# Eight of 56 precomputed parts moved from the traces of block 0 to its tails, in a fused four-layer residual kernel

## What is computed

```python
# layer 0: gated multi-scale traces
wg     = sigmoid(concat(x, ema(x)) @ Wg + bg);  gated = x * wg
h1     = gelu(x @ Wn1 + bn1)                     # 64 wide
mod    = 0.5 + sigmoid(h1 @ Wn2 + bn2)           # 16 numbers for each token
traces = [ema_d(gated * mod[:, d]) for d in range(16)]
gate   = sigmoid(sum_d(traces[d] * blend[d]) @ Wtemp + btemp)
soma   = gelu(x @ Wsoma + bsoma)
x      = x + layernorm((soma * gate) @ Wout)
# layer 1: tanh scores, masked softmax over tokens, pooling
x      = x + softmax(mask + tanh(x @ W1 + b1) @ v) @ x / count
# layer 2: eight gated experts and a shared one (SiLU), all of them for every token
# layer 3: x + gelu(x @ W1 + b1) @ W2, with an expert's columns picked for each sequence
```

## Time and profile before

| | us |
|---|---|
| median of the three runs | 2813.46 |
| their lowest and highest | 2812.75, 2815.56 |
| the profiled execution, its own time | 2811.08 |
| its span in the trace | 2809.3 |
| TensorE busy | 2771.3 (99%) |
| VectorE, ScalarE, GpSimd busy | 1786.2, 1450.2, 1207.1 |

### The profile page before, as it was taken

How to read it: one execution, slowest core, us unless ns; L and a number is a source line. 1 busy time by engine, 2 the same in 40 slices (tenths; PEclk the granted TensorE clock), 3 DMA queues, 4 the chain that set the end, 5 groups by cost and what they waited for, 6 DMA issues and landing times.

```text
span 2809.3 us, 36696 instructions
## 1 busy us (share of the span) xinstructions
PE 2771.3 (99%) x12794; PEld 2301.0 (82%) x12794; DVE 1786.2 (64%) x2976; ACT 1450.2 (52%) x2625; POOL 1207.1 (43%) x950
## 2 busy tenths in 40 slices
PE   8799999999999999999999999999999999999999
PEld 5588888888888888888888888888888888888888
DVE  8698778867777666566765766555766563333443
ACT  4455666566456544554545644455644563333445
POOL 5256435633554345424543345433454333333334
PEclk9899999999999999999999999999999999999999
DMA  4244333433222322112321222211322131111221
GB/s 154 73 151 127 97 105 105 142 99 102 80 68 95 111 68 68 57 59 68 105 64 59 81 89 73 68 48 57 111 79 63 44 103 45 46 45 46 79 89 58
DMA packets 117383, 230.37 MB, mean 82 GB/s; under 512 B 13672, under 2 KB 58960, under 8 KB 117200
## 3 DMA queue, kind: packets, MB, share of 16 engines
q1 hardware_dynamic: 81808, 190.15, 21.3%
q10 hardware_dynamic: 32832, 29.49, 4.3%
q0 software_dynamic: 2560, 8.39, 0.9%
HBM read 219.89 MB, written 8.09 MB: 81 GB/s over the span
## 4 chain that ended last, share of the span: by engine, by line
PE 94%; DVE 4%; issue 1%; ACT 1%; DMA 0%; SPq 0%; ACTq 0%; DVEq 0%
PE bank L587 20%; PE bank L588 20%; PE bank L589 20%; PE ps_out L587 10%; PE ps_out L589 10%; PE ps_out L588 10%; PE bank L580 1%; DVE trace L1137 1%; DVE trace L1129 1%; PE bank L708 0%; DVE w_lo L1209 0%; PE bank L699 0%; DMA pre_x<-in_xT 0%; PE bank L694 0%; DVE hid L1243 0%
## 5 line engine op out<-in xcount | busy, mean ns | idle before, releaser
L1382 POOL TENSOR_TENSOR hid_lo<-hid,hid_hi 128x512 fp32r<-128x512 f32 x640 | 848.3, 1326 | 1547.7 <-ACT hid_hi L1014 1547.3
L587 PE MATMUL bank<-res_lo,w_hi 128*128 128x512 f32 x2432 | 956.6, 393 | 5.1 <-DVE res_lo L1228 2.3
L588 PE MATMUL bank<-res_hi,w_lo 128*128 128x512 f32 x2432 | 947.7, 390 | 0.0
L589 PE MATMUL bank<-res_hi,w_hi 128*128 128x512 f32 x2432 | 946.8, 389 | 0.0
L1243 DVE TENSOR_TENSOR hid<-hid,bank 128x512 f32<-128x512 f32 x576 | 394.6, 685 | 637.0 <-PE bank L589 611.4
L983 ACT ACTIVATE hid<-bank 128x512 f32<-128x512 f32 x576 | 344.1, 597 | 586.4 <-PE bank L589 585.8
L1209 DVE TENSOR_TENSOR w_lo<-w_raw,w_hi 128x768 fp32r<-128x768 f32 (+2 forms) x520 | 485.2, 935 | 194.9 <-ACT w_hi L945 152.1
L945 ACT ACTIVATE w_hi<-w_raw 128x768 fp32r<-128x768 f32 x392 | 331.3, 845 | 482.2 <-PE ps_out L589 470.6
L587 PEld LDWEIGHTS bank<-res_lo,w_hi 128*128 128x128 f32 x2432 | 456.9, 188 | 97.4 <-issue 4.6
L589 PEld LDWEIGHTS bank<-res_hi,w_hi 128*128 128x128 f32 x2432 | 456.6, 188 | 97.1
L588 PEld LDWEIGHTS bank<-res_hi,w_lo 128*128 128x128 f32 x2432 | 457.0, 188 | 89.5
(11 more groups left out here) (180 smaller groups left out, 1569.4 us busy)
## 6 DMA issues: line engine op xcount, KB each, us to landing
w_raw<-in_chunks SPq DMA_DIRECT2D x392, 384.0 KB, 3.1
mod_on<-mod_rows ACTq DMA_DIRECT2D x154, 128.0 KB, 3.2
w_raw<-in_head_chunks SPq DMA_DIRECT2D x64, 224.0 KB, 2.5
stat<-mod_rows ACTq DMA_DIRECT2D x70, 128.0 KB, 3.1
x_in<-in_xT SPq DMA_DIRECT2D x16, 256.0 KB, 3.8
pre_x<-in_xT SPq DMA_DIRECT2D x14, 256.0 KB, 7.2
soma_rows<-pre_soma SPq DMA_DIRECT2D x14, 256.0 KB, 2.0
soma<-soma_rows SPq DMA_DIRECT2D x14, 256.0 KB, 3.7
```

The lines of the kernel that those rows point to most:

```text
L587: mm(out, wh, xl, start=start and i == 0, stop=False, skip_group_check=not lone)
L588: mm(out, wl, xh, start=False, stop=False, skip_group_check=not lone)
L589: last = mm(out, wh, xh, start=False, stop=end, skip_group_check=not lone)
L1382: nc.gpsimd.tensor_tensor(hid_lo[i % DEPTH][:], hid[i % 3][:], f(hid_hi[i % DEPTH][:]), ALU.subtract).then_inc(s_hlo, 1)
```

## The change

Eight parts leave the trace pieces of lane 1 (each of lane 1's trace pieces that falls in the second half of the interleaving now gets one part, not two; "j >= 12" counts pieces). The parts of the later units slide back accordingly, and the last eight, units 12 and 13, are placed by a new table `PARTS_AT` after tail pieces. The small ("setup", "bias") entry goes from behind lane 1's piece 37 to behind lane 0's piece 46, since its matmul waits for all the parts.

```diff
-          (1, 33): [("cut", 2)], (1, 37): [("setup", "bias")], (0, 40): [("cut_lo", 2)], (0, 41): [("cut", 3)],
+          (1, 33): [("cut", 2)], (0, 46): [("setup", "bias")], (0, 40): [("cut_lo", 2)], (0, 41): [("cut", 3)],
           (1, 40): [("cut_lo", 3)]}
 EARLY = 4
+
+PARTS_AT = {(1, 37): 1, (0, 40): 2, (1, 38): 1, (1, 39): 1, (0, 43): 1, (1, 40): 1, (0, 45): 1}
...
-        for _ in range((1 if j < 12 and s == 0 else 2) if 7 <= j < 7 + ND else 0):
+        for _ in range((1 if j < 12 and s == 0 or j >= 12 and s else 2) if 7 <= j < 7 + ND else PARTS_AT.get((s, j), 0)):
```

## The result

The changed kernel takes 2817.53 us (median of 20 runs, 2815.94 to 2820.15) against 2812.98 us of the kernel before in the same measurement (20 runs). The ratio is 1.0016 with a 95% interval of 1.0010 to 1.0022: 4.5 us slower. The profiled execution took 2816.60 us, 5.5 more than the profiled one of before.

A forecast was written before the change was run, and what follows sets the result against it. A chain through three engines in the tails was taken to set the first front's time. ScalarE's loads (+2.9) and the last pooling's clock (+1.6) gave +4.5 us, 2818.0 on the median; range 2813.0 to 2821.0.

The forecast's parts named there:

- The number: Whole kernel: +4.5 us against the kernel before, 2818.0 us on the median; this forecast was given a chance of 0.46.
- What bounds it: the first front's time: TensorE's long stream after block 0 is left alone, so only the first front's time, 119.04 us into the span, can move.
- Leaving the traces: 0: Lane 1's trace pieces: VectorE's 2.07 us a piece covers the parts, so fewer parts there change nothing; taken as 0.
- after 84.5: Sign of a wrong forecast: VectorE's last multiply of the traces standing later than 84.5 us, against 84.19 before.
- Four loads, the first hidden, three on the chain: +2.9: ScalarE in the tails: four more table loads from alternating Gelu with Tanh and Exp; lane 1's pooling starts 2.9 us later.
- Lane 0's pooling at the higher clock: Tails, TensorE: parts keep it busy up to lane 0's pooling, which takes 1.99 us instead of 3.78, starting at 112.3.
- The clock at the last pooling: +1.6: Lane 1's pooling on TensorE: little work before it lowers the clock, so 3.6 us instead of 1.99; range down to 0.
- The rival at the end of the traces: Lane 1's last trace pieces: TensorE at 1.2 GHz delays part 11/2 and gate matmul, +2.5 on top (+7.0); chance 0.12.
- The rival of dearer switches: ScalarE in the tails: each exposed table switch costs more than its load, 1.9 us on top (+6.4); chance 0.08.
- The rival "no load is exposed": ScalarE in the tails: Gelu, Tanh and Exp served without switches, giving -0.2 to -1.8 us; chance 0.10.

The follow-up runs named there:

- the second measurement: The changed kernel run again unaltered, with another profile taken, against the kernel before: 2817.38 us against 2813.62, ratio 1.0012.
- Experiment 4: The changed kernel with the part ahead of lane 1's last mix put behind trace piece 22: 2816.26 us against 2813.64 for the kernel before, ratio 1.0011.
- Experiment 1: The changed kernel with Tanh in place of Gelu in the parts of units 12 and 13: 2811.76 us against 2813.64 for the kernel before, ratio 0.9996.
- experiments 2 and 3: 2: kernel before plus two one-column Gelus (four loads), 2814.50 us against 2813.64. 3: changed kernel, Tanh for Gelu in unit 13's parts, 2811.67 us against 2813.62.

## Why the prediction was right, point by point

- *The number.* +4.5 forecast, +4.55 measured; the measurement's interval is 2.8 to 6.2 us, and the second measurement gave +3.8. The agreement to 0.1 us is luck.
- *What bounds it: the first front's time.* Right in the main: the yardstick gives +4.4 us. A small cost lies ahead of it, at the end of the traces.
- *Leaving the traces: 0.* Too small. I had the last mix 0.2 us later and VectorE 0.1; the mix was 0.5 later, and VectorE 0.3 in the first profile and 1.0 in the second. The last multiply stood at 84.59, and "after 84.5" was one of my own signs of being wrong. Experiment 4 shows that it is on time when part 11/2 doesn't stand ahead of the mix. What the forecast had wrong is the clock there: it took the spacings of the rows at 2.4 GHz, and the two parts ahead of 11/2 ran at 1.2 (four records in 1.97 and 1.91 us). Only the rival below reckoned with that.
- *Four loads, the first hidden, three on the chain: +2.9.* The four loads came where they were put, at 101.82, 106.29, 109.91 and 113.23. In the stretch lane 1's pooling starts 2.84 us later than before in the first profile, and only 1.27 in the second, where the projection and the matmul behind it ran at the higher clock; so +2.9 is right for tails whose first part is as slow as before, and the first profile was that. Experiment 1 gives 3.2 us for the loads against the same kernel without them. The reason was too simple, though: experiments 2 and 3 show that the same loads cost 0.7 us without the parts, and that the one ahead of lane 0's Exps costs 0.4. It isn't the loads by themselves but two of them, in a stretch that the parts had filled, that are the price. In the sum this came out right because it was followed step by step with both in it.
- *Lane 0's pooling at the higher clock.* Right: 1.99 us, and later than before all the same (112.92, predicted 112.3).
- *The clock at the last pooling: +1.6.* Right as a size, and only half as a place. The first profile shows it at the front (4.69 us instead of 3.11, 1.6) and has 1.99 us at the pooling itself, the second shows it at both (another 1.66). What I missed is that the start of the tails can get faster: lane 0's projection and the gate matmul behind it, from the start of the one to the start of what follows the other, took 5.07 us before, 5.24 in the first profile and 3.56 in the second. In the second profile these two misses, 1.5 us one way and 1.6 the other, cancel. That the sum is right there too (+4.5) is luck.
- *The rival at the end of the traces.* Its condition came true in part. The granted clock was 0.50 from 75 to 80 us, with TensorE busy 4.66 of these 5.00 us, and it was back for part 11/2 (1.05 us) in the first profile, only late in it (1.71) in the second, and for the gate matmul (1.89) in both. So 0.3 and 1.0 us came of its 2.5. The argument against it held for the gate matmul.
- *The rival of dearer switches.* Fell: 1.29 to 1.30 us each.
- *The rival "no load is exposed".* The four loads are there and two of them are exposed, so it fell. Experiment 1 makes its condition true: -1.9 us, the end of the span that I gave it (-0.2 to -1.8).

## What to carry to other kernels

Before work is moved into idle time, look at whose idle time it is on every engine the work touches: here TensorE had gaps to spare, but ScalarE's were where table switches would have hidden, and the moved work brought the switches with it. Keep activations of one table together, and where a chain of small steps leaves TensorE at its lower clock, first try a few matmuls that nobody waits for. Ten of them gained 3.5 us by the median (ratio 0.9991, 0.9982 to 1.0000), and 5.0 together with three parts placed where they needed no load (0.9981, 0.9972 to 0.9990). And take more than one profile before a place of low clock is read as the kernel's own.

## What the runs showed of the hardware that I had not expected

- The same instructions in the same order run at the low clock in different places in different executions: in the two profiles of the changed kernel the projection took 2.80 and 1.99 us, the gate matmul behind it 2.82 and 1.89, lane 1's pooling 1.99 and 3.65. The stretch as a whole was 40.31 and 40.39 us.
- Two costs that were small or negative alone (+0.7 and -2.0 us) were +4.4 together.
